# An expert layer, an attention layer and an expert layer on one core: other group sizes, another order of the queues, repeated waits left out

## The reference

```python
x = x + 0.5 * ffn(layernorm(x))      # layer 1
x = x + attn(layernorm(x))           # layer 2
x = x + 0.5 * ffn(layernorm(x))      # layer 3, the weights of layer 1

ffn:  shared = (silu(x @ sg.T) * (x @ su.T)) @ sd.T               # 256 hidden
      probs  = sigmoid(x @ router.T + bias)                       # 8 experts
      scores, idx = top_k(probs, 2); scores /= sum(scores)
      out = shared + sum over the two experts of score * ((silu(x @ gate_e) * (x @ up_e)) @ down_e)
attn: q, k, v, o_gate = x @ Wq.T, x @ Wk.T, x @ Wv.T, x @ Wg.T    # 8 heads of 16, q and k with rotary embedding
      o = (q.(k^T v)*scale + sum v) / (q.sum k*scale + 512) + conv5(v)
      out = (o * o_gate) @ Wo.T
```

## Time and profile before

| what | us |
|---|---|
| median of three executions | 570.14 |
| lowest and highest | 568.78 and 574.89 |
| the profiled execution, its own time | 569.31 |
| its span, first to last instruction | 567.5 |

### The profile page before, as it was taken

The page is one execution under the profiler, slowest core; times in us unless marked ns, Lnnn a source line. Parts: engine busy times, 40 slices in busy tenths (PEclk is TensorE's granted clock), DMA queues, the critical chain, the costliest instruction groups (busy, mean ns, idle before and its releaser), DMA issues.

```text
span 567.5 us, 11032 instructions
## 1 busy us (share of the span) xinstructions
PE 486.3 (86%) x3056; PEld 402.5 (71%) x3056; DVE 353.9 (62%) x1059; ACT 280.6 (49%) x630; POOL 334.7 (59%) x338
## 2 busy tenths in 40 slices
PE   0958489999899999999999996989899998999920
PEld 0847478777777878888778775877787776778720
DVE  4688775633557675778887878788756353344331
ACT  4714346554655657556664465554364554355300
POOL 4355864076788676527788768735775764460072
PEclk9979799999999999999999999999999999999985
DMA  8931143243341333023213321123334434341121
GB/s 230 369 105 33 44 134 103 79 119 87 81 145 34 94 84 103 11 68 96 71 52 112 99 76 42 43 84 87 101 103 142 116 105 114 108 111 44 43 59 52
DMA packets 76041, 53.69 MB, mean 95 GB/s; under 512 B 9776, under 2 KB 70832, under 8 KB 75984
## 3 DMA queue, kind: packets, MB, share of 16 engines
q1 hardware_dynamic: 67792, 36.19, 22.0%
q0 software_dynamic: 8192, 16.79, 10.7%
HBM read 27.39 MB, written 25.56 MB: 93 GB/s over the span
## 4 chain that ended last, share of the span: by engine, by line
PE 74%; DVE 8%; issue 7%; ACT 4%; POOL 3%; DMA 2%; POOLq 0%; SPq 0%; DVEq 0%; ACTq 0%
PE gu L835 14%; PE gu L793 8%; PE ht_ps L826 7%; PE gu L795 7%; PE gu L794 7%; PE ht_ps L846 4%; PE gu L753 4%; PE gu L754 4%; PE gu L755 4%; PE xt_ps L776 3%; POOL yg L1145 2%; PE misc L855 2%; ACT gs L973 1%; PE misc L915 1%; PE misc L868 1%
## 5 line engine op out<-in xcount | busy, mean ns | idle before, releaser
L1145 POOL DMA_INDIRECT yg<-y_sorted,places x128 | 123.8, 967 | 107.0 <-PE gu L795 40.5
L1124 POOL DMA_INDIRECT x_sorted<-xn,places x128 | 128.5, 1004 | 84.5 <-PE gu L795 34.5
L835 PEld LDWEIGHTS gu<-w,hT 128*128 128x128 f32 x736 | 92.3, 191 | 24.0 <-issue 19.4
L835 PE MATMUL gu<-w,hT 128*128 x736 | 102.0, 281 | 6.2 <-ACT hT L979 4.0
L973 ACT ACTIVATE gs<-gu 128x512 f32<-128x512 f32 (+1 forms) x128 | 74.3, 582 | 63.7 <-PE gu L755 39.1
L793 PE MATMUL gu<-w,xbt_hi 128*128 x184 | 85.7, 466 | 6.8 <-ACT ys L954 3.9
L1192 DVE TENSOR_TENSOR hs<-gs,gu 128x512 f32<-128x512 f32 x96 | 63.2, 662 | 34.7 <-ACT gs L973 29.4
L1178 DVE TENSOR_TENSOR xbt_lo<-xt_ps,xbt_hi 128x256 fp32r<-128x256 f32 x96 | 39.4, 410 | 62.3 <-ACT xbt_hi L962 61.5
L795 PE MATMUL gu<-w,xbt_hi 128*128 x184 | 73.2, 398 | 0.0
L794 PE MATMUL gu<-w,xbt_lo 128*128 x184 | 73.2, 398 | 0.0
L979 ACT ACTIVATE hT<-ht_ps 128x512 f32<-128x512 f32 x96 | 55.6, 580 | 35.1 <-PE ht_ps L826 33.3
(11 more groups left out here) (132 smaller groups left out, 862.9 us busy)
## 6 DMA issues: line engine op xcount, KB each, us to landing
xb<-x_sorted SPq DMA_DIRECT2D x88, 128.0 KB, 2.2
y_sorted<-ys SPq DMA_DIRECT2D x88, 128.0 KB
X<-x_dram SPq DMA_DIRECT2D x8, 256.0 KB, 5.9
x_sorted<-yg SPq DMA_DIRECT2D x4, 512.0 KB, 6.7
x_sorted<-xn,places POOLq DMA_INDIRECT x128, 2.3
yg<-y_sorted,places POOLq DMA_INDIRECT x128, 2.6
out_dram<-X SPq DMA_DIRECT2D x8, 256.0 KB, 2.3
raw<-gate_w_dram SPq DMA_DIRECT2D x4, 256.0 KB, 4.6
```

What stands on the lines that cost most here:

```text
L835: mm = pe.matmul(dst[:, j * D:(j + 1) * D], hT[r % 2][:, at:at + P], w_flat[:, bass.ds(expert[r][j] + 2 * GU + half * D, D)], start=half = ...
L1124: nc.gpsimd.indirect_dma_start(x_sorted[l, g], bass.IndirectOffsetOnAxis(places[l, g][:, k, t:t + 1], 0), xn[:, b, t % T], None).then_inc( ...
L1145: nc.gpsimd.indirect_dma_start(yg[slot][:, k, t], None, y_sorted[l, g], bass.IndirectOffsetOnAxis(places[l, g][:, k, at:at + 1], 0)).then_ ...
```

## The change

1. `GROUPS`: layer 1 has groups of 2, 3 and 3 batches, layer 3 of 2, 3, 2 and 1. What is sized by the largest group grows with it: the two rooms from 23 to 31 blocks, and their zeroing from 6 to 8 transfers.
2. `XB`, the number of buffers for loaded pairs, falls from 6 to 5.
3. The lengths in the planner are other ones, nearly all shorter; `HOP` goes from 14 to 16; `v_tok` is planned behind `k_tok`.
4. `search` calls the list schedule 600 times. Each trial adds random shifts (normal, with a deviation of 1.2) to the rank of some families of pieces (a family is a kind of piece in a layer, for one batch or group), starting from the best trial so far, and the shortest plan is kept.
5. `Once`: on each engine, a wait on a semaphore for a value that the engine has already waited for is not issued.

No engine instruction that computes is changed; the tiles of routing vectors follow the group size.

```diff
-GROUPS = {1: ((0, 2), (2, 4), (4, 6), (6, 8)), 3: ((0, 2), (2, 4), (4, 6), (6, 8))}
+GROUPS = {1: ((0, 2), (2, 5), (5, 8)), 3: ((0, 2), (2, 5), (5, 7), (7, 8))}
-XT, XB, HB, YB, GB, YG, ROOMS = 6, 6, 4, 3, 3, 3, 2
-PACE, HOP, NEAR = 140, 14, 10
+XT, XB, HB, YB, GB, YG, ROOMS = 6, 5, 4, 3, 3, 3, 2
+PACE, HOP, NEAR = 140, 16, 10
+ROUNDS, SEED = 600, 1
...
-        self.schedule()
+        self.search()
...
-        op(("stats", l, b), "DVE", 125, *needs, ("moments", l, b - 1) if b else None)
-        op(("moments", l, b), "DVE", 95, ("stats", l, b))
+        op(("stats", l, b), "DVE", 80, *needs, ("moments", l, b - 1) if b else None)
+        op(("moments", l, b), "DVE", 50, ("stats", l, b))
...
-        op(("norm", l, b, 0), "ACT", 98, ("shift", l, b), *free)
+        op(("norm", l, b, 0), "ACT", 80, ("shift", l, b), *free)
...
-            self.op(("front", u, 1), "PE", 70, *needs)
+            self.op(("front", u, 1), "PE", 73, *needs)
...
-        self.op(("silu", u), "ACT", 60, ("front", u, 0))
-        self.op(("hid", u), "DVE", 69, ("silu", u))
+        self.op(("silu", u), "ACT", 50, ("front", u, 0))
+        self.op(("hid", u), "DVE", 60, ("silu", u))
...
-        op(("count", l, g), "PE", 70, ("choose", l, g), ("cut_earlier",))
+        op(("count", l, g), "PE", 35, ("choose", l, g), ("cut_earlier",))
...
-            op(("add", l, b, "first"), "DVE", 155, ("gather", l, b, 2 * T - 1), ("weigh", l, g))
+            op(("add", l, b, "first"), "DVE", 106, ("gather", l, b, 2 * T - 1), ("weigh", l, g))
...
-            op(("tap", b, j), "DVE", 80, ("tap", b, j - 1) if j > 1 else ("conv0", b))
+            op(("tap", b, j), "DVE", 64, ("tap", b, j - 1) if j > 1 else ("conv0", b))
...
+    def family(self, key):
+
+        return (key[0], *key[1][0:3]) if key[0] in ("front", "silu", "hid") else key[0:3]
+
+    def search(self):
+
+
+        serial = {key: n for n, key in enumerate(self.ops)}
+        plain = {key: (self.urgency(key), self.stage(key), serial[key]) for key, o in self.ops.items() if o[0]}
+        family = {key: self.family(key) for key in plain}
+        families = sorted(set(family.values()), key=str)
+        rng = np.random.default_rng(SEED)
+        best, shift = None, {}
+        for n in range(ROUNDS):
+            trial = dict(shift)
+            if n:
+                for i in rng.integers(len(families), size=rng.choice((1, 3, 10, 40))):
+                    trial[families[i]] = rng.normal(0, 1.2) if rng.random() < 0.8 else 0
+            rank = {key: (u + trial.get(family[key], 0), *more) for key, (u, *more) in plain.items()}
+            if self.schedule(rank) and (best is None or max(self.end.values()) <= best[0]):
+                best, shift = (max(self.end.values()), rank), trial
+        self.schedule(best[1])
...
+        class Once:
...
+            def __init__(self, eng):
+                self.eng, self.reached = eng, {}
+
+            def wait_ge(self, s, value):
+                if value > self.reached.get(s, 0):
+                    self.reached[s] = value
+                    self.eng.wait_ge(s, value)
...
         @block.tensor
         def _(pe):
+            once = Once(pe)
...
-                pe.wait_ge(xb_loaded[r % XB], 16 * (r // XB + 1))
-                wait(pe, xbt_lo_done, r)
+                once.wait_ge(xb_loaded[r % XB], 16 * (r // XB + 1))
+                wait(once, xbt_lo_done, r)
```

More of the change, by code:

```diff
@@ L466, in schedule @@
                     best = (t, serial[key], key, engine, t)
-            assert best, ("no piece can begin", sorted(waiting, key=str)[:20])
+            if not best:
+                return False
             _, _, key, engine, t = best
@@ L676, in _ @@
         def _(sp):
+            once = Once(sp)
             def load_x(b):
@@ L682, in load @@
                 if n == 0:
-                    sp.wait_ge(scattered[l, g], 16 * 2 * tiles(l, g))
-                wait(sp, xbt_ready, r - XB + 1)
+                    once.wait_ge(scattered[l, g], 16 * 2 * tiles(l, g))
+                wait(once, xbt_ready, r - XB + 1)
                 k = width(l, g, n)
@@ L829, in down @@
             def down(r):
-                pe.wait_ge(hT_done, r + 1)
+                once.wait_ge(hT_done, r + 1)
                 dst = bank(("R", r))[:, 0]
@@ L965, in silu @@
                 n = nth_hidden[u]
-                act.wait_ge(gu_ready, nth_unit[u] + 1)
-                wait(act, h_done, n - GB + 1)
+                once.wait_ge(gu_ready, nth_unit[u] + 1)
+                wait(once, h_done, n - GB + 1)
                 if u[0] == "R":
@@ L975, in hT_copy @@
             def hT_copy(r):
-                act.wait_ge(hT_ready, r + 1)
-                wait(act, y_ready, r - 1)
+                once.wait_ge(hT_ready, r + 1)
+                wait(once, y_ready, r - 1)
                 n = width(*plan.pair[r]) * I
@@ L1071, in _ @@
         def _(pool):
+            once = Once(pool)
             half = DK // 2
@@ L1080, in rope_cos @@
             def rope_cos(b):
-                pool.wait_ge(k_copied, b + 1)
-                wait(pool, kv_ready, b)
+                once.wait_ge(k_copied, b + 1)
+                wait(once, kv_ready, b)
                 nc.gpsimd.tensor_tensor(heads(k_rot[:], 0, DK), heads(k_tok, 0, DK), table(cost, 0, DK), ALU.mult)
@@ L1107, in pace @@
                 half_through, through = plan.through(key)
-                wait(pool, half_ready, half_through)
-                wait(pool, gu_ready, through)
+                wait(once, half_ready, half_through)
+                wait(once, gu_ready, through)
             def scatter(l, g, n):
@@ L1202, in add @@
                 if step == "shared":
-                    dve.wait_ge(shared_ready, nth_shared[l, b] + 1)
-                    wait(dve, updated[b], update(l, b, "shared") - 1)
+                    once.wait_ge(shared_ready, nth_shared[l, b] + 1)
+                    wait(once, updated[b], update(l, b, "shared") - 1)
                     v.scalar_tensor_tensor(out=flat(X[:, b]), in0=ht_ps[:], scalar=0.5, in1=flat(X[:, b]),
@@ L1395, in mask_kv @@
                 src = misc("kv", b)
-                dve.wait_ge(kv_ready, b + 1)
-                wait(dve, num_ready, b)
+                once.wait_ge(kv_ready, b + 1)
+                wait(once, num_ready, b)
                 v.tensor_tensor(kv_bd[:], src[:, 0:D], bmask[:], ALU.mult)
```

352 lines of the change are left out of this document (177 added, 175 removed).

## The result

The changed kernel takes 548.36 us (median of four executions, 544.9 to 551.7) against 571.58 for the kernel before, run beside it on the same chip (four executions, 568.78 to 574.89). The ratio is 0.9585, with a 95% interval of 0.954 to 0.963: 4.1% faster. The forecast was 539.5, 9 us too low; the time lies inside the range, at the place of the rivals A and D (548.5 and 549).

The account below looks back on a forecast made before the run. PE was taken to bound the kernel from 80 to 540 us, GpSimd's gathers the end. Span 567.5 - 12.0 - 9.5 - 9 = 537.0 us, plus 1.8 and 0.8, gave 539.6, stated as 539.5; range 520 to 558.

Parts of the forecast that it names:

- A: Whole kernel: blocks and end gain as counted, order gives nothing; 548.5 us; chance 0.25 together with D.
- D: Kernel's end: gathers of batches 5 and 6 hold GpSimd's queue, tail not shortened; 549 us; chance 0.25 with A.
- the copies: Middle stretch, within the blocks term: 4 pairs fewer save 4 x 0.42 = 1.7 us of uncovered ScalarE copies.
- Blocks: Routed products on PE: 177 blocks instead of 184, 10.3 us less work and 1.7 of copies; -12.0 us.
- The end: Behind the last routed store: 8 gathers instead of 16, 10.1 us less; term -9.5, bounds -10.1 and 0.
- some 23: Sign that the forecast is right: some 23 us from the last store to the end instead of 32.
- rival C: Handover to layer 3's second group of three batches: PE hole of 6 to some 30 us; 578.5 us; chance 0.08.
- Order: PE's idle time, by new lengths, 600 trials and HOP: -9 us, 4 at the beginning and 5 in the middle.
- any search should touch: Argument against A: PE's 11.6 us wait for ScalarE's norm at the start is plain enough for any search.
- Waits and buffers: Repeated waits, zeroing and one load buffer fewer: 0 each; bounds -4.6 for waits, +6.8 zeroing, +7 buffer.
- B: Start and middle: early waits and half the middle's idle time go, order about -27; 521.5 us; chance 0.22.
- The shift of 1.26 us: A 128x4 shift, group mean 0.277 us, cited for VectorE and GpSimd excluding each other, making the order term about 0.

## Why the prediction was right or wrong

**What bounds the kernel** was right: PE's work and its idle time at the start and the end. The direction and the range held, but the forecast's sum of -30.5 on the span came out as -20.6. In the terms of the sum: PE's work fell by 4.8 us where 10.3 were forecast; the end, 16.4 us shorter behind the last routed product with 10.9 us of work moved ahead of it, is worth 5.5 net where 9.5 were; and PE's idle time up to the last routed product fell by 10.3 us, where 9 for the order and 1.7 for the copies were. So some 5.5 us are missing in the work and 4 at the end.

**Blocks, -12.0.** 177 products, as counted. As work the term was good between the two runs that differ in these blocks alone: 9.4 us against 10.3. From the kernel before to the changed one PE's busy time fell by only 4.7. The clock does not account for that, since over the span it was 0.965 before and 0.97 after. How much the order alone can do is shown by two pairs of runs with the same matmuls, 473.9 us without the search against 481.6 (clock 0.982 and 0.97), and 497.0 with the old groups against 486.3. Why the new order costs PE this work stays open. One profile of each is little for it: the changed kernel with all its waits, the same plan, had 479.6.

**The end, -9.5, is a step that failed.** The tail itself went as forecast and better: from the last store to the end 32.4 to 19.2 us ("some 23" was named). What the prediction put at nothing is PE's work beside it. Its first part said that shared work fits there, without its length: it was 7.87 us behind the last store, and in the changed kernel it is 0. The prediction's own rival C had the mechanism: 55 us of the handover must be filled with shared and attention work. Of these, by its numbers, 49 were at hand, so some 6 us of work were lacking. The sum of the forecast has no term for that lack. In the changed kernel PE hardly idles there (2.4 of 57.3 us), but the 7.87 us that lay beside the tail are gone. The table in the section on the result shows that the two go together in every run; that the one is the cause of the other is my reading. How much the one-batch group is worth by itself was not measured; layer 3's grouping as a whole is worth 3 to 6 us. (A slip beside it: by the prediction's own numbers the bound -12.8 of the blocks is 10.3/0.94 + 1.7 = 12.6.)

**Order, -9.** In size it was about right in the changed kernel: PE idles 10.3 us less up to the last routed product. It lay elsewhere: 8.4 at the start, where 4 were counted, and 1.9 in the middle, where 5 were. The longest wait of PE for ScalarE's norm, which "any search should touch", is still there and even a little longer, 12.3 us where it was 11.6. In total these waits fell from 18.3 us to 13.7, so they gave 4.6 of the 8.4; in the changed kernel's waits up to 80 us (us in total, times, longest):

```profile
PE misc L896 <- ACT xn L1039: 13.7, 2, 12.3
```

The waits for the shared expert's hidden values gave 6.0 (10.0 to 4.0), and others took 2.2 back. The term also does not stand by itself, as the prediction's "order" had it: with the old groups it is 0 (ratio 1.0016).

**The terms do not add up.** With the new lengths, nothing is gained without new groups (0.2% slower), 3.0% with layer 1's, 3.7% with layer 3's, and 4.1% with both. By the sum, both together should have given 6.8% (0.9697 x 0.963 / 1.0016 = 0.932). The changed kernel's 44 us without a routed product are where a part of the gain goes, by my reading: neither half of the grouping alone has them (20.6 and 16.7 us), both together do, and the work beside the tail is gone. That was not shown by a run that removes the hole alone.

**Waits and buffers, 0.** The waits are right, by a run that issues them all. Zeroing and the smaller `XB` were not tried by themselves.

**Rivals.** A said that the order gives nothing: wrong in the changed kernel, although its time is met. D, a tail not shortened because of GpSimd's queue, is wrong: 1.67 us are free between the two groups of gathers. That the time came out like A's and D's is luck. C was right as a mechanism with the old lengths, 61 us without a routed block, and near in its price, in part by luck (above). In the changed kernel its stretch is 44 us long, near the 55 that C worked out, and full of other work; so it costs no idle time there, but what it leaves undone at the end. B, some 27 us from the order, did not come: 10.3 us of idle time went.

**Operations slowed beside each other.** The shift of 1.26 us is of the kind that the run with the cut on VectorE shows. Taken away at one place, the start, it gives nothing that can be measured; what it costs at all the others together was not tried.

## What to carry to other kernels

Before a serial tail is priced by its own length, add up the work of the bounding engine that lies beside it, and ask whether the new plan needs that same work as a filler elsewhere: what covers a hole in the middle is missing at the end. Group sizes and the order of work are one choice: here the groups alone cost 2.8%, the order alone gave nothing, and both gave 4.1%, so try them together and look for the longest stretch without the main work. Measure the lengths from a trace first: with the new groups they brought 36 us, 16 of them a loss made good, and six hundred trials on top of them 3.6.

## What was not expected of the hardware

**Equal instructions, other busy times.** With the same 2985 matmuls PE was busy for 473.9 us in one order and 481.6 in another, and with the same 3056 for 486.3 and 497.0. The granted clock is part of it. In the changed kernel it is 0.50 of full, the 1.2 GHz level, for 3.4 us at a time from 303.0, 326.9 and 344.0 us; just before, PE had waited for 0.89 us (up to 302.8), 3.37 (up to 327.0) and 1.06 (up to 341.8). A wait of 0.87 us up to 271.8 brought no such fall, so what brings it is not shown. Behind the one of 3.37 us, PE's timeline shows products of 0.63 us, where the line's mean is 0.40; the 20 us around them have a granted clock of 0.91:

```profile
327.00 0.79 PE L834 MATMUL gu<-w,xbt_hi 128*128 x1 [3.37 <-DVE raw L1431]
327.58 0.63 PE L835 MATMUL gu<-w,xbt_lo 128*128 x1
328.01 0.63 PE L836 MATMUL gu<-w,xbt_hi 128*128 x1
```

```profile
320.00:340.00 20.00, 16.41 (x86) 12.82 (x85) 18.38 (x44) 8.24 (x18) 14.13 (x15) 0.91 0.09 30
```

Since neighbours overlap in these records, their distances say it better: 0.43 us from one product to the next here, against the 0.23 of the earlier trace rows at the full 2.4 GHz.

**Chips differ by 15%.** The kernel before takes 569 to 572 us on one and 650 to 656 on another, and not evenly: between the same pair of kernels the ratio was 1.0281 on one and 0.9846 on the other. On the chip with the longer times the chain of the groups alone (start, us, what) has gaps in the middle of straight PE work in which nothing that the profile shows was waited for:

```profile
617.93 0.83 issue
...
621.42 1.71 issue
623.13 0.98 PE gu L835 x7
624.11 5.87 issue
```

The routed products between them keep their steps of 0.23 us. PE's idle time between the first and the last routed product was 94 us there and 43.9 in the other run of the same kernel. What fills these gaps is open.
